# Longer VectorE instructions and a bounds check on the scatters in a gated attention and mixture-of-experts kernel

## The reference: what is computed

```
s = attention over columns:  q, k, v = xn Wq, xn Wk, xn Wv;  softmax(qT k / sqrt(8)) over the 256 columns, times vT, times Wo
scores = softmax(xn @ gate.T)                  # 32 experts in 8 groups of 4
3 groups by their best score, then 6 experts of these; their weights are normalised to a sum of 1
y = sum over the 6 of weight_e * (silu(xn @ w1_e.T) * (xn @ w3_e.T)) @ w2_e.T      # hidden size 128
shared = (silu(xn @ sw1.T) * (xn @ sw3.T)) @ sw2.T                                # hidden size 256
out = x + s * silu(y + shared)
```

## Time and profile before

| | us |
|---|---|
| median of 3 runs | 614.14 (613.87 to 614.29) |
| the profiled execution | 614.29 |
| its span, first to last instruction | 612.4 |
| PE busy | 529.6 (86%) |
| DVE busy | 495.9 (81%) |
| POOL busy | 388.1 (63%) |
| POOL, 192 scatters of line 433 | 189.2, mean 986 ns |
| POOL, 192 gathers of line 451 | 196.8, mean 1025 ns |

### The profile page before, as it was taken

One profiled execution on the slowest core, in us unless ns is written; L12 is line 12 of the kernel. 1 busy time (PEld: TensorE's weight loads), 2 busy tenths in 40 slices (PEclk: granted clock), 3 DMA queues, 4 the chain that ended last, 5 costly groups with the idle time before them and its releaser, 6 DMA issues.

```text
span 612.4 us, 14022 instructions
## 1 busy us (share of the span) xinstructions
PE 529.6 (86%) x3756; PEld 444.6 (73%) x3756; DVE 495.9 (81%) x1460; ACT 358.5 (59%) x730; POOL 388.1 (63%) x401
## 2 busy tenths in 40 slices
PE   7859898989898999522999999999999999999970
PEld 6447676767676777412999998888888888888850
DVE  6996988898989889830555579999998999999995
ACT  5535656565757465411666666666666666666650
POOL 1077767777777777772000477767777767777773
PEclk9879898989898999875999999999999999999995
DMA  9999995969695543665366899999999999999984
GB/s 310 419 393 386 399 363 228 338 239 341 243 340 210 181 172 121 237 105 179 123 197 197 249 308 349 326 331 335 335 350 327 349 320 347 336 347 332 341 262 150
DMA packets 128713, 174.78 MB, mean 285 GB/s; under 512 B 12290, under 2 KB 113410, under 8 KB 127746
## 3 DMA queue, kind: packets, MB, share of 16 engines
q1 hardware_dynamic: 104706, 108.29, 52.2%
q0 software_dynamic: 18432, 50.36, 24.8%
q10 hardware_dynamic: 5504, 15.24, 6.5%
HBM read 81.56 MB, written 92.27 MB: 284 GB/s over the span
## 4 chain that ended last, share of the span: by engine, by line
PE 57%; DVE 27%; POOL 5%; issue 5%; DMA 2%; ACT 2%; POOLq 0%; ACTq 0%; DVEq 0%; SPq 0%
PE ps L765 24%; PE ps L753 9%; PE ps L785 8%; POOL slots_d L433 5%; PE ps L662 4%; DVE w_all L964 4%; PE ps L775 4%; PE ps L654 4%; PE ps L670 3%; DVE work L1056 3%; DVE stats L805 2%; DVE xnT L858 1%; DVE top L841 1%; DVE mx L984 1%; DVE acc L1039 1%
## 5 line engine op out<-in xcount | busy, mean ns | idle before, releaser
L451 POOL DMA_INDIRECT early<-slots_d,slot_at x192 | 196.8, 1025 | 127.0 <-PE ps L775 63.1
L433 POOL DMA_INDIRECT slots_d<-early,slot_at x192 | 189.2, 986 | 88.5 <-issue 56.4
L765 PE MATMUL ps<-w_all,work 128*128 x1344 | 166.3, 274 | 0.0
L765 PEld LDWEIGHTS ps<-w_all,work 128*128 128x128 f16 x1344 | 130.5, 98 | 15.8
L1056 DVE SCALAR_TENSOR_TENSOR work<-ps,work 128x512 f16<-128x512 f32 x112 | 76.7, 685 | 44.0 <-ACT work L582 44.0
L785 PE MATMUL ps<-w_all,work 128*128 x672 | 91.7, 273 | 1.2 <-DVE work L1069 1.2
L753 PE MATMUL ps<-ident,work 128*128 128x128 f32 x448 | 70.0, 279 | 25.0 <-DMA work<-slots_d 19.8
L589 ACT ACTIVATE work<-ps 128x256 f32<-128x256 f32 x112 | 43.0, 384 | 75.4 <-PE ps L765 75.4
L582 ACT ACTIVATE work<-ps 128x512 f16<-128x512 f32 x112 | 66.5, 593 | 28.2 <-PE ps L753 28.1
L1039 DVE SCALAR_TENSOR_TENSOR acc<-early,wk,acc 128x256 f32<-128x256 f32 x160 | 77.1, 482 | 4.1 <-DMA early<-slots_d,slot_at 0.6
L611 ACT ACTIVATE early<-ps 128x512 f32<-128x512 f32 x112 | 66.9, 597 | 17.7 <-PE ps L785 17.2
(11 more groups left out here) (147 smaller groups left out, 738.3 us busy)
## 6 DMA issues: line engine op xcount, KB each, us to landing
work<-slots_d SPq DMA_DIRECT2D x112, 256.0 KB, 4.8
slots_d<-early SPq DMA_DIRECT2D x112, 256.0 KB
slots_d<-pad SPq DMA_DIRECT2D x7, 3072.0 KB, 22.2
w_all<-in_wexp ACTq DMA_DIRECT2D x7, 1536.0 KB, 10.0
slots_d<-work SPq DMA_DIRECT2D x1, 5120.0 KB, 19.4
s_all<-in_x SPq DMA_DIRECT2D x8, 512.0 KB, 5.5
ysh_d<-work ACTq DMA_DIRECT2D x8, 512.0 KB, 8.6
early<-ysh_d SPq DMA_DIRECT2D x32, 128.0 KB
```

Of the source, the lines that this page charges most:

```text
L433: pool.indirect_dma_start(slots_d[:, :], bass.IndirectOffsetOnAxis(ap=slot_at[:, at:at + 1], axis=0), xn[b % XN_RING][:, t, :], None).then ...
L451: pool.indirect_dma_start(gath[:, at % GATH_RING, :], None, slots_d[:, :], bass.IndirectOffsetOnAxis(ap=slot_at[:, rank_of(at):rank_of(at) ...
L765: mm = pe.matmul(ps[:, 2 + p % 2, h * 2 * I:(h + 1) * 2 * I], xT[p % 2][:, x_low, h, k, :], w16[:, bass.ds(at + (w_low * WEXP + k * 2 * I) ...
```

## The change

Three edits. The low weights of an expert are computed in one instruction of 768 columns in place of three of 256, and those of the last four experts in two instructions of 1536 columns in place of twelve of 256; the counts of the semaphore `s_wlo` follow this. In `weigh` the comparison is one instruction of 768 columns in place of two of 384, and so is the product. And the scatters carry a bounds check, as the gathers of line 451 already do: a slot over SLOTS - 1 would be skipped, without an error.

```diff
--- before.py
+++ after.py
@@ -46,7 +46,6 @@
 XN_RING = 3
 BATCH_ROWS = TB * TOP_K
 WEXP = HC * 2 * I + H
-PART = 256
 EB = E // B
 HALF = EB // 2
 
@@ -345,7 +344,7 @@
             sp.wait_ge(s_at, 2 * B)
             for k in range(2):
                 sp.wait_ge(s_ysh[k], 16 * (B // 2))
-            sp.wait_ge(s_wlo, B * EB)
+            sp.wait_ge(s_wlo, (B - 1) * EB + 2)
 
             def rows_of_pair(p):
                 return slots_d[p * (2 * P):(p + 1) * (2 * P), :].rearrange("(h p) c -> p h c", p=P)
@@ -431,7 +430,8 @@
                         at = b * BATCH_ROWS + t * TOP_K + k
                         let_pass(b, t * TOP_K + k)
                         pool.indirect_dma_start(slots_d[:, :], bass.IndirectOffsetOnAxis(ap=slot_at[:, at:at + 1], axis=0),
-                                                xn[b % XN_RING][:, t, :], None).then_inc(s_disp[b % XN_RING], 16)
+                                                xn[b % XN_RING][:, t, :], None, bounds_check=SLOTS - 1,
+                                                oob_is_err=False).then_inc(s_disp[b % XN_RING], 16)
 
 
             stored = 0
@@ -731,7 +731,7 @@
 
 
             pe.wait_ge(s_tables, 16)
-            pe.wait_ge(s_wlo, B * EB)
+            pe.wait_ge(s_wlo, (B - 1) * EB + 2)
             pe.wait_ge(s_at, 2 * B)
             pe.wait_ge(s_y, 2 * B)
 
@@ -926,13 +926,11 @@
 
                 def every_rank(v):
                     return by(v, E).unsqueeze(2).to_broadcast([P, TB, TOP_K, E])
-                for t in range(0, TB, 2):
-                    dve.tensor_tensor(ranked[:, t:t + 2], every_rank(pos)[:, t:t + 2],
-                                      top8[:, t:t + 2, 0:TOP_K].unsqueeze(3).to_broadcast([P, 2, TOP_K, E]), ALU.is_equal)
+                dve.tensor_tensor(ranked, every_rank(pos), top8[:, :, 0:TOP_K].unsqueeze(3).to_broadcast(
+                    [P, TB, TOP_K, E]), ALU.is_equal)
                 then(dve.tensor_tensor(wts, masked, sel, ALU.mult))
                 dve.tensor_reduce(row1[:], by(wts, E), AX_X, ALU.add)
-                dve.tensor_tensor(ranked[:, 0:2], ranked[:, 0:2], every_rank(wts)[:, 0:2], ALU.mult)
-                then(dve.tensor_tensor(ranked[:, 2:4], ranked[:, 2:4], every_rank(wts)[:, 2:4], ALU.mult))
+                then(dve.tensor_tensor(ranked, ranked, every_rank(wts), ALU.mult))
                 then(dve.tensor_scalar(row2[:], row1[:], 1e-20, W_UP, ALU.add, ALU.mult))
                 dve.reciprocal(row3[:], row2[:])
                 then(dve.tensor_reduce(to, by(by_rank, E), AX_X, ALU.add))
@@ -958,24 +956,18 @@
                 dve.scalar_tensor_tensor(hT_s[:, m, :], ps[:, 5 + 2 * m, :], 1.0 / (X_UP * W_UP), silu_s[m],
                                          ALU.mult, ALU.mult).then_inc(s_h, 1)
 
-            def low_part(low, raw, high):
-                for c in range(WEXP // PART):
-                    part_of = slice(c * PART, (c + 1) * PART)
-                    ins = dve.scalar_tensor_tensor(low[:, part_of], raw[:, part_of], W_UP, high[:, part_of],
-                                                   ALU.mult, ALU.subtract)
-                ins.then_inc(s_wlo, 1)
-
             def low_weights(b):
                 dve.wait_ge(s_whi, b + 1)
                 for e in range(EB):
-                    low_part(weights_of(b, 1)[:, e], raw_weights(b)[:, e], weights_of(b, 0)[:, e])
+                    dve.scalar_tensor_tensor(weights_of(b, 1)[:, e], raw_weights(b)[:, e], W_UP, weights_of(b, 0)[:, e],
+                                             ALU.mult, ALU.subtract).then_inc(s_wlo, 1)
 
             def low_weights_last():
                 for k in range(2):
                     dve.wait_ge(s_whi, B + k)
-                    for e in range(HALF):
-                        low_part(weights_of(B - 1, 1)[:, k * HALF + e], raw_last[k][:, e],
-                                 weights_of(B - 1, 0)[:, k * HALF + e])
+                    dve.scalar_tensor_tensor(weights_of(B - 1, 1)[:, k * HALF:(k + 1) * HALF], raw_last[k], W_UP,
+                                             weights_of(B - 1, 0)[:, k * HALF:(k + 1) * HALF],
+                                             ALU.mult, ALU.subtract).then_inc(s_wlo, 1)
 
             def batch(b):
                 hidden(b, 0)
```

## The result

The changed kernel takes 621.41 us in the median of four runs (620.7 to 621.97), against 614.21 for four runs of the kernel before: the ratio is 1.0115, with an interval of 1.010 to 1.013. The forecast was slower, 626.9, range 617.5 to 630.5. The profiled execution took 620.72 us, its span is 619.0, 6.6 more than before.

A forecast was written before the change was run, and what follows sets the result against it. POOL, issuing scatters late from 87 us on, was taken to bound the first stage. Terms 7.3 + 4.9 + 1.2 + 1.8 - 2.45 gave 12.8 us over the median 614.14: 626.9, range 617.5 to 630.5.

The forecast's parts named there:

- bounds check, 192 scatters: POOL's scatters: the check adds 0.038 us to each, read from gathers that carry one; 7.3 us in all.
- low weights, seven stretches: Scatters beside 768-column instructions wait for later borders: 0.70 us more in each of seven four-expert stretches, 4.9 us.
- low weights, last four experts: Two 1536-column instructions hold scatters for 1.44 us against 0.22 now: plus 1.2 us.
- weigh: Scatters beside the 768-column comparison and product wait 0.44 us a batch against 0.21: 0.23 more, eight times, 1.8 us.
- waits given back: POOL's two waits, at scatters 34 and 42, disappear in full: 0.58 and 1.87, 2.45 us back.
- What bounds the kernel: First stage ends when POOL has issued its 192 scatters; behind 87 us, POOL's gains or losses move the second stage one for one.
- The rule of the end of the DVE instruction: A scatter waits until 0.11 us before the end of the running DVE instruction, only with two SBUF inputs.
- B: Rival: the 0.038 us belongs to gathers and the check is free; waits shrink rather than vanish; +6.0, 620.1; chance 0.20.
- A: Rival: check and long DVE instructions both cost as predicted; 626.9, own range 623 to 630.5; chance 0.50.
- C: Rival: the check costs, but a long DVE instruction lets POOL in before its end; +4.9, 619.0; chance 0.12.
- The cover of the `xn` buffers: Third `xn` buffer stays free in time for ACT's batch 7, some 3.6 us earlier; cover shrinks from 16 to 6 us.
- D: Rival, faster: the check is free and POOL gets in as today; chain before 87 us 0.8 shorter; 613.3; chance 0.08.

The follow-up runs named there:

- the run with one input: The changed kernel with the first 28 experts' low weights computed from one SBUF input, the subtraction left out: 616.11 us, ratio 1.0020 against the kernel before.
- the run that only changes the gathers: The kernel before without the bounds check on the gathers of the second stage: 614.16 us, ratio 0.9998.

## Why the prediction was right, and where its sizes were not

The last scatter's end moved by 6.8 us: the last scatter ends at 286.46 + 0.97 = 287.43, before at 279.69 + 0.96 = 280.65. By the terms of the sum:

| term | predicted | measured in the two traces |
|---|---|---|
| bounds check, 192 scatters | 7.3 | 192 x 0.013 = 2.5 |
| first scatter's start | 0 | 31.12 for 30.72: 0.4 |
| low weights, seven stretches | 4.9 | excess 1.62 to 6.29: 4.7 |
| low weights, last four experts | 1.2 | 0.22 to 1.14: 0.9 |
| weigh | 1.8 | 1.69 to 1.41: -0.3 |
| other scatters | 0 | 1.40 to 1.96: 0.6 |
| waits given back | -2.45 | 2.49 to 0.69: -1.8 |
| sum | 12.8 | 7.0, of which rounding takes 0.2 |

Two rows of the changed kernel's timeline, shortly before weigh begins at 239.90, to which the paragraph on weigh refers:

```profile
237.97 0.38 DVE L910 TENSOR_TENSOR early<-early 128x128 f32<-128x128 f32 x1
238.06 1.15 POOL L432 DMA_INDIRECT slots_d<-early,slot_at  x1 [0.30 <-issue]
```

And two of the kernel before, for the paragraph on the rule:

```profile
76.01 0.23 DVE L870 CAST sel<-early 128x128 bf16<-128x128 f32 x1
76.07 1.00 POOL L433 DMA_INDIRECT slots_d<-early,slot_at  x1 [0.30 <-issue]
```

- **What bounds the kernel: right.** PE and DVE idle before the border, POOL's last scatter sets it, the second stage keeps its length; leaving out `let_pass` gained what the waits held.
- **The rule of the end of the DVE instruction: right** for instructions with two SBUF inputs, from 256 to 3072 columns, to a few hundredths of a microsecond. "Only instructions with two tensor inputs in SBUF do this" was too much: the run with one input has scatters 0.51 and 0.42 us too long, and even in the kernel before a cast with one input holds one by 0.04, near the rule's 76.01 + 0.23 - 76.07 - 0.11 = 0.06 (the second pair of rows above). The changed instructions all have two, so the sum didn't suffer. The seven stretches came out at 0.90 us each for a predicted 0.96. The VectorE instructions of 768 columns had the predicted length.
- **The bounds check: the mis-sized term,** 4.8 of the 5.6 us by which the sum was too high. The step was "I take 0.038, as these are the nearest rows". A gather and a scatter of the same bytes differ by themselves (947 and 960 ns without a check), and the check costs them different amounts (51 and 13 ns). (The shortest scatter rose by 16 ns, the median by 13; the difference, 0.6 us, is in the table's other scatters.) The upper bound was a fair bound, but minimum and median having the same gap was no evidence for either end.
- **weigh: wrong.** The step "A first scatter meets the comparison in two cases of three" fails: POOL's phase is not free. In the changed kernel the last scatter to start before weigh does so 0.26, 0.38 or 0.69 us ahead of it in seven of the eight batches, and in the run with weigh alone three batches in a row show 0.03, 0.00 and 0.00 us beside weigh. What may set these places stands a little ahead of weigh: instructions with two SBUF inputs, of which line 910 in the first pair of rows above holds a scatter by 0.18 us, 1.9 us before weigh. That this coupling is the reason is argued from these rows and was not tried by itself. Over the five profiled kernels with long instructions the excess beside weigh is 1.1 to 1.8 us, over the nine with short ones 1.2 to 2.9: no cost of the long ones shows.
- **The first scatter's start: noise.** It is at 31.12 with the check alone too, but at 30.77 with the check and all edits without `let_pass`, and at 31.31 in the run that only changes the gathers.
- **The waits: partly right.** With the check at 13 ns POOL was ready for scatter 42 at 86.1, not at 87.5, and what it waited for there let it go at 86.68, 0.44 us earlier than before and not 0.8; so 0.7 us of waits stayed. The actual case lies between B (620.1) and A of the rivals, nearest to B, whose condition, a check that costs nothing, is nearly what the runs show, and which had a chance of 0.20. That the time fell inside the range is owed to its width: the range was drawn from a little under C up.
- **The cover of the `xn` buffers: held, as predicted,** but DVE's chain was only 1.3 us ahead at batch 7 (ACT normalises at 203.30, before at 204.63, and waits for DVE), not 3.6.
- **The rival on the other side (D) and the fixed cost per instruction:** the changed DVE is busy 5.0 us less (490.9, before 495.9), near the 4.8 that the prediction worked out for seven batches, and it bought nothing.

## What to carry to other kernels

Ask of a faster engine who shares a resource with it, and which of the two is late: here DVE's instruction count fell and the kernel lost 7 us, because POOL, 8.5 us late, pays for long DVE instructions with two SBUF inputs that run when it issues. Where POOL issues DMAs back to back, look at how its distances fall on multiples of DVE's start-to-start time, and measure before going shorter as well as longer: 256 columns was better than 128, 192, 384, 768 and 3072. A price read from another kind of transfer is a bound, not a value.

## What the runs showed of the hardware that was not expected

A train of short DVE instructions can be worse for POOL than one long one: at 128 columns (0.28 us each, starts 0.20 apart) and at 192 (0.35, 0.27) each of the eight trains holds one scatter to its end, up to 3.6 us, after none to two got in at borders, while at 256 (0.42, 0.34) a scatter gets in at each border. By the rule of 0.11 us before an instruction's end there would be an opening of about 0.03 us in all three (an estimate: 0.11 less the 0.08 by which one instruction reaches into the next), so the opening's length alone does not explain it; what closes it is open. The check on an indirect DMA costs 51 ns on a gather and 13 ns on a scatter. A VectorE instruction with one SBUF input can hold a scatter (0.51 us beside the `tensor_scalar` of 768 columns), a reduction with one does not (0.96 us, plain, beside 0.71 us of it). The Trainium skill (SBUF — State Buffer, "SBUF: two separate sides") has the lock held for the whole instruction: the runs agree for 256 columns and more, and below that find it held over instruction borders.
